# The experts' down product of a mixture-of-experts layer as plain fp32 matmuls from unsplit weights

## What is computed

```
h   = silu(x @ w0[e]) * (x @ w1[e])     # 128 -> 512
y   = h @ wo[e]                         # 512 -> 128
out = sum over the two chosen experts of g * y
x   = layernorm(x + out)
```

## Time and profile before

| | |
|---|---|
| median of 3 runs | 411.37 us (410.9 to 412.04) |
| the profiled execution | span 414.5 us; no other time is recorded for it |
| PE busy | 349.5 us, 84% (weight loads 238.0) |
| DVE busy | 292.3 us, 71% |
| ACT busy | 235.2 us, 57% |
| POOL busy | 230.4 us, 56% |
| granted TensorE clock | 0.98 of full speed over the span |

### The profile page before, as it was taken

The page is one execution under the profiler, slowest core; times in us unless marked ns, Lnnn a source line. Parts: engine busy times, 40 slices in busy tenths (PEclk is TensorE's granted clock), DMA queues, the critical chain, the costliest instruction groups (busy, mean ns, idle before and its releaser), DMA issues.

```text
span 414.5 us, 9020 instructions
## 1 busy us (share of the span) xinstructions
PE 349.5 (84%) x2869; PEld 238.0 (57%) x2869; DVE 292.3 (71%) x836; ACT 235.2 (57%) x460; POOL 230.4 (56%) x341
## 2 busy tenths in 40 slices
PE   1999977888988999988878899988997999999900
PEld 1666645556544545444444445567776899898800
DVE  3555645888788888878796736376776877877737
ACT  2677644432667666455577687744644665666514
POOL 2660598855354435271569788546575445445525
PEclk9999999999999999999999999999999999999975
DMA  8933322636515040322624343211112211111054
GB/s 269 336 110 106 87 85 77 187 94 186 171 33 166 5 140 5 99 70 75 196 69 131 117 155 102 74 32 40 53 41 78 78 53 40 53 52 35 32 171 146
DMA packets 44461, 41.97 MB, mean 101 GB/s; under 512 B 4560, under 2 KB 38416, under 8 KB 44416
## 3 DMA queue, kind: packets, MB, share of 16 engines
q1 hardware_dynamic: 41136, 35.10, 28.1%
q0 software_dynamic: 2272, 4.69, 3.2%
q10 hardware_dynamic: 1008, 1.61, 1.1%
HBM read 26.36 MB, written 14.75 MB: 99 GB/s over the span
## 4 chain that ended last, share of the span: by engine, by line
PE 56%; DVE 20%; issue 7%; POOL 7%; ACT 4%; another core or an unknown queue 3%; DMA 2%; ACTq 0%; DVEq 0%; POOLq 0%
PE banks L1017 12%; DVE nm L1210 8%; PE banks L1044 6%; PE banks L1032 4%; PE banks L859 4%; PE banks L698 4%; PE banks L907 3%; PE banks L1045 2%; PE banks L755 2%; PE banks L937 2%; PE banks L763 2%; DVE ctx_in L1152 2%; PE banks L806 2%; PE banks L934 1%
## 5 line engine op out<-in xcount | busy, mean ns | idle before, releaser
L1210 DVE TENSOR_REDUCE nm<-banks 128x4 f32<-128x1024 f32 x64 | 78.1, 1220 | 17.5 <-PE banks L850 11.4
L1520 ACT ACTIVATE probs_all<-banks 128x1024 f32<-128x1024 f32 x64 | 65.4, 1023 | 36.0 <-PE banks L859 29.6
L1017 PE MATMUL banks<-w_split,scores_in 128*128 x234 | 64.5, 410 | 0.0
L1342 DVE TENSOR_TENSOR ctx_in<-ctx_in,banks 128x512 f32<-128x512 f32 x39 | 26.8, 687 | 27.3 <-ACT ctx_in L1567 21.4
L1017 PEld LDWEIGHTS banks<-w_split,scores_in 128*128 128x128 f32 x234 | 40.8, 189 | 7.7 <-issue 0.9
L1705 POOL DMA_INDIRECT slots_dram<-rows,place_u x32 | 31.9, 996 | 23.5 <-DVE count L1302 16.1
L1727 POOL DMA_INDIRECT y_dram<-x,scatter_u x39 | 38.5, 987 | 11.4 <-POOL x L1723 9.7
L1567 ACT ACTIVATE ctx_in<-banks 128x512 f32<-128x512 f32 x39 | 23.3, 599 | 36.7 <-PE banks L1017 31.9
L859 PE MATMUL banks<-scores_in 32*128 32x256 f32 x256 | 32.2, 326 | 12.0 <-ACT probs_all L1520 6.0
L1044 PE MATMUL banks<-w_split,scores_in 128*128 x156 | 39.1, 327 | 2.8 <-ACT scores_in L1573 2.1
L907 PE MATMUL banks<-probs_all,vals 128*9 128x256 f32 x512 | 39.7, 381 | 0.2
(11 more groups left out here) (230 smaller groups left out, 802.2 us busy)
## 6 DMA issues: line engine op xcount, KB each, us to landing
scores_in<-k_dram SPq DMA_DIRECT2D x32, 128.0 KB, 2.7
scores_in<-q_dram SPq DMA_DIRECT2D x32, 128.0 KB, 2.7
ctx_in<-in_L_ffn_w SPq DMA_DIRECT2D x16, 256.0 KB, 2.7
cs_wide<-cs_dram SPq DMA_DIRECT2D x14, 256.0 KB, 3.7
scores_in<-slots_dram SPq DMA_DIRECT2D x39, 65.0 KB, 1.9
k_dram<-split_qk SPq DMA_DIRECT2D x8, 256.0 KB, 2.5
q_dram<-split_qk SPq DMA_DIRECT2D x8, 256.0 KB, 2.3
ctx_in<-in_L_ffn_wo SPq DMA_DIRECT2D x8, 256.0 KB, 2.9
```

What stands on the lines that cost most here:

```text
L1017: m = TE.matmul(up_bank(i, j), xT[:, i % XT, xh, :], all_weights[:, c + j * FF:][:, bass.ds(expert_at[i], FF)], start=n == 0, stop=n == 2)
L1210: V.tensor_reduce(most, maxima_of(n).rearrange("p (j k q) -> p j k q", j=2, k=TPS), AX_X, ALU.max, negate=True).then_inc(s["nmax"], 1)
L1520: C.activation(probs(n).rearrange("p j k q -> p (j k q)"), EXPS, ACT.Exp, scale=SCALE).then_inc(s["probs"], 1)
```

## The change

Only w0 and w1 are split (16 pieces); wo is loaded as it is, by a DMA for each expert into a buffer of its own (`load_down` into `w_down`), in the steps in which (n - 32) % 3 is 2, so that a step either splits a piece or loads a wo. The hidden is transposed and copied once, unsplit, by ACT; DVE's copy of the rest is gone. `down` is 4 plain fp32 matmuls of 128 columns, and waits for all of `w_down`. DVE makes the tile's result in one operation from the bank: times g, plus x2 out of `xg`; ACT's and POOL's operations are gone, and POOL only scatters. Before the last three `down`, `turn_hidden` of the last tile comes first. `hsT` has a buffer of its own.

```diff
-W_HEAD, W_REST, W_OUT, W_ALL = 0, 2 * FF, 4 * FF, 6 * FF
+W_HEAD, W_REST = 0, 2 * FF
+UP_ALL = 4 * FF // FF
 W_RING = NT * D // FF
-PIECES = 3 * NE
+PIECES = 2 * NE
 XG, AHEAD = 8, 4
-LAST_ADDED = SLOT_TILES - 3
 XT, TURNED_AHEAD, DOWN_LAG, HS = 3, 2, 3, 3
...
+        if i == SLOT_TILES:
+            second.append(("turn_hidden", i - 1))
         if i >= DOWN_LAG:
             second.append(("down", i - DOWN_LAG))
         if i + TURNED_AHEAD < SLOT_TILES:
             second.append(("turn_x2", i + TURNED_AHEAD))
-        if 1 <= i <= SLOT_TILES:
+        if 1 <= i < SLOT_TILES:
             second.append(("turn_hidden", i - 1))
...
-            yield "split_weights", piece
-            if W_RING <= piece + 2 < PIECES:
-                yield "load_weights", piece + 2
-            piece += 1
+        elif n >= LAST_MIXER + 6 and piece + whole_pieces < PIECES + NE:
+            if (n - LAST_MIXER) % 3 == 2:
+                yield "load_down", whole_pieces
+                whole_pieces += 1
+            else:
+                yield "split_weights", piece
+                if W_RING <= piece + 2 < PIECES:
+                    yield "load_weights", piece + 2
+                piece += 1
...
-        w_split = sb("w_split", [P, NE, W_ALL], F32R)
+        w_split = sb("w_split", [P, NE, UP_ALL * FF], F32R)
+        w_down = sb("w_down", [P, NE, FF])
+        hsT = sb("hsT", [P, HS, FF])
...
-            y, turned = bank(6 + i % 2)[:, 0:2 * D], bank(6 + i % 2)[:, 2 * D:3 * D]
+            y, turned = bank(6 + i % 2)[:, 0:D], bank(6 + i % 2)[:, D:2 * D]
...
-                q.wait_ge(s["y_x2"], i - XG + 1)
+                q.wait_ge(s["y_add"], i - XG + 1)
...
+            def load_down(e):
+                mixer_left()
+                SY.dma_start(w_down[:, e, :].rearrange("p (c d) -> p c d", c=FC),
+                             A["L0_ffn_wo"][e].rearrange("(c p) d -> p c d", p=P)).then_inc(a["w_down"], 16)
...
-                                      all_weights[:, c + j * FF:][:, bass.ds(expert_at[i], FF)], start=n == 0, stop=n == 2)
+                                      all_up[:, c + j * FF:][:, bass.ds(expert_at[i] * UP_ALL, FF)], start=n == 0, stop=n == 2)
...
             def down(i):
-                slot = i % HS
                 yb, _ = shared(i)
-                q.wait_ge(s["hsT_hi"], i + 1)
-                q.wait_ge(s["hsT_lo"], i + 1)
+                q.wait_ge(s["hsT"], i + 1)
+                q.wait_ge(a["w_down"], 16 * NE)
                 q.wait_ge(s["xT_lo"], min(i + 2 * TURNED_AHEAD + 1, SLOT_TILES))
                 q.wait_ge(s["y_add"], i - 1)
                 for c in range(FC):
-                    w = all_weights[:, W_OUT + 2 * c * D:][:, bass.ds(expert_at[i], 2 * D)]
-                    TE.matmul(yb[:, 0:2 * D], hsT[:, slot, 0, c * P:(c + 1) * P], w, start=c == 0, stop=False)
-                    m = TE.matmul(yb[:, 0:D], hsT[:, slot, 1, c * P:(c + 1) * P],
-                                  all_weights[:, W_OUT + 2 * c * D:][:, bass.ds(expert_at[i], D)],
-                                  start=False, stop=c == FC - 1)
+                    m = TE.matmul(yb, hsT[:, i % HS, c * P:(c + 1) * P], all_down[:, c * D:][:, bass.ds(expert_at[i], D)],
+                                  start=c == 0, stop=c == FC - 1)
                 m.then_inc(s["down_mm"], 1)
...
-            def turn_hidden(i):
-                slot = i % 2
-                q.wait_ge(s["hsT_hi"], i + 1)
-                q.wait_ge(s["down_mm"], i - HS + 1)
-                V.tensor_tensor(hsT[:, i % HS, 1, :], hidden_bank(i), hsT[:, i % HS, 0, :].bitcast(F32),
-                                ALU.subtract).then_inc(s["hsT_lo"], 1)
...
-                q.wait_ge(s["y_half"], i + 1)
+                q.wait_ge(s["down_mm"], i + 1)
+                q.wait_ge(a[f"g{i % XG}"], 16 * (i // XG + 1))
                 q.wait_ge(a[f"y_out{i % Y_RING}"], 16 * (i // Y_RING))
-                V.scalar_tensor_tensor(y_slot[:, i % Y_RING, :], shared(i)[0][:, 0:D], xg[:, i % XG, ROW_WEIGHT:ROW], y_half[:, i % 2, :],
+                V.scalar_tensor_tensor(y_slot[:, i % Y_RING, :], shared(i)[0], xg[:, i % XG, ROW_WEIGHT:ROW], xg[:, i % XG, 0:D],
                                        ALU.mult, ALU.add).then_inc(s["y_add"], 1)
-                if i >= LAST_ADDED:
-                    y = y_slot[:, i % Y_RING, :]
-                    q.wait_ge(s["y_add"], i + 1)
-                    V.tensor_tensor(y, y, xg[:, i % XG, 0:D], ALU.add).then_inc(s["y_last"], 1)
 
...
-                e, i = divmod(n, 3)
-                raw = w_raw[:, n % W_RING, :]
-                if i < 2:
-                    head = w_split[:, e, W_HEAD + i * FF:W_HEAD + (i + 1) * FF]
-                else:
-                    raw = raw.rearrange("p (c d) -> p c d", c=FC)
-                    head = w_split[:, e, W_OUT:].rearrange("p (c h d) -> p c h d", c=FC, h=2)[:, :, 0, :]
+                e, i = divmod(n, 2)
                 q.wait_ge(a[f"e{n % W_RING}"], 16 * (n // W_RING + 1))
-                C.activation(head, raw, ACT.Identity).then_inc(s["w_hi"], 1)
+                C.activation(w_split[:, e, W_HEAD + i * FF:W_HEAD + (i + 1) * FF], w_raw[:, n % W_RING, :],
+                             ACT.Identity).then_inc(s["w_hi"], 1)
...
-                C.activation(hsT[:, i % HS, 0, :], hidden_bank(i), ACT.Identity).then_inc(s["hsT_hi"], 1)
-
-            def down(i):
-                q.wait_ge(s["down_mm"], i + 1)
-                q.wait_ge(s["y_add"], i - 1)
-                q.wait_ge(a[f"g{i % XG}"], 16 * (i // XG + 1))
-                C.activation(y_half[:, i % 2, :], shared(i)[0][:, D:2 * D], ACT.Identity, scale=xg[:, i % XG, ROW_WEIGHT:ROW]).then_inc(s["y_half"], 1)
+                C.activation(hsT[:, i % HS, :], hidden_bank(i), ACT.Identity).then_inc(s["hsT"], 1)
...
-                y = y_slot[:, i % Y_RING, :]
-                if i < LAST_ADDED:
-                    q.wait_ge(s["y_add"], i + 1)
-                    G.tensor_tensor(y, y, xg[:, i % XG, 0:D], ALU.add).then_inc(s["y_x2"], 1)
-                    q.wait_ge(s["y_x2"], i + 1)
-                else:
-                    q.wait_ge(s["y_last"], i - LAST_ADDED + 1)
+                q.wait_ge(s["y_add"], i + 1)
                 G.indirect_dma_start(
                     y_dram[:, :], bass.IndirectOffsetOnAxis(ap=scatter_u[:, i:i + 1], axis=0),
-                    y, None).then_inc(a[f"y_out{i % Y_RING}"], 16)
+                    y_slot[:, i % Y_RING, :], None).then_inc(a[f"y_out{i % Y_RING}"], 16)
 
             G.memset(minus_half[:, :], -0.5).then_inc(s["consts_g"], 1)
```

More of the change, by code:

```diff
@@ L266, in middle_order @@
 def middle_order():
-    piece = 0
+    piece = whole_pieces = 0
     for n in range(FIRST_STEP, NPAIR):
@@ L293, in middle_order @@
                 yield "load_weights", i
-        elif n >= LAST_MIXER + 6 and piece < PIECES:
-            yield "split_weights", piece
-            if W_RING <= piece + 2 < PIECES:
-                yield "load_weights", piece + 2
-            piece += 1
+        elif n >= LAST_MIXER + 6 and piece + whole_pieces < PIECES + NE:
[7 more added lines that the diff above has]
+                piece += 1
         yield from tiles_step(n)
@@ L327 @@
     "r2 ln2_var ln2_in ln2 x2 x2_t x2T rows_x2 gate_mm logit ge topped chosen rank_mm counted w_hi w_lo "
-    "xg_t xT_hi xT_lo up_mm sil hid turn_mm hsT_hi hsT_lo down_mm y_half y_add y_x2 y_last "
+    "xg_t xT_hi xT_lo up_mm sil hid turn_mm hsT down_mm y_add "
     "end_var end_in end_scaled end_ln out_act out_dve"
@@ L472, in build @@
         w_raw = work.rearrange("p (r n) -> p r n", n=FF)
-        y_slot, y_half = x1[:, 0:Y_RING, :], x1[:, Y_RING:Y_RING + 2, :]
-        to_slots = x1[:, Y_RING + 2, 0:SLOT_TILES]
+        y_slot = x1[:, 0:Y_RING, :]
+        to_slots = x1[:, Y_RING, 0:SLOT_TILES]
         flat_q = scores_in[:, :, :, :].rearrange("p n r s -> p (n r s)")
@@ L1005, in expert_of @@
                 q.wait_ge(s["steps_v"], tile_ready(i))
[L1006 removed]
+                expert_at[i] = TE.value_load(tile_at[0:1, 0, i:i + 1], min_val=0, max_val=(NE - 1) * FF)
             def up(i):
@@ L1027, in turn_hidden @@
                 q.wait_ge(s["av_hi"], B)
-                q.wait_ge(s["hsT_lo"], i if i < TURNED_ALONE else i - 1)
+                q.wait_ge(s["hsT"], i if i < TURNED_ALONE else i - 1)
                 if i == TURNED_ALONE:
@@ L1380, in vector_program @@
                           rank_tiles=rank_tiles, place_tiles=place_tiles,
-                          up=up, turn_hidden=turn_hidden, turn_x2=turn_x2, down=down)
+                          up=up, turn_x2=turn_x2, down=down)
             for stage, *at in middle_order():
```

39 lines of the change are left out of this document (15 added, 24 removed).

## The result

The changed kernel takes 405.26 us in the median of 4 runs (404.54 to 405.73), the kernel before 411.55 (410.9 to 412.04, 4 runs): a ratio of 0.9842, 95% interval 0.9827 to 0.9858, some 6.3 us less. I had forecast 410.4 with a range down to 408.4. Some executions of each kernel run with a lower granted clock and take over 1.5% longer; the ratios here leave them out, the medians in us do not.

The account below looks back on a forecast made before the run. The prediction took TensorE to bound the loop's steady part. Its terms, +0.8 - 0.75 - 0.3 - 0.7 = -0.95 us, turned the median of 411.37 into 410.4 us, range 408.4 to 412.4.

Parts of the forecast that it names:

- Product: `down` in each of 39 turns: eight records take 0.89 us, 0.02 more than before, +0.8 us in all.
- Rivals C: `down`: first weight load not issued ahead under `up`, 0.1 us per turn, +3.9 us, 414.3; chance 0.08.
- D: `down`: bound by columns, not weight loads; 128 more per chunk cost +9.8 us, 419.4; chance 0.03.
- Start of the loop: First 14 tiles: two waits of TensorE on DVE and ACT shrink, -0.75 us together, bounds 0 and -2.
- the wait before L947: TensorE near 295 us, waiting for DVE's table behind the 0.68 us subtraction: the 0.5 us wait goes.
- the 0.25 us at 313 us: ACT leaves a stall with L1579 at 313.28; without L1579, `down` at 314.48 starts 0.25 us sooner.
- Weights: Splitting steps: ACT and POOL lose eight pieces each and buffers fill earlier, -0.3 us, bounds 0 and -2.
- the ring: Four weight buffers delay ACT, 1.4 us in all, 0.42 before an exponential; with 16 pieces they fill earlier.
- The steady part: Loop bound by TensorE: work taken off DVE, ACT and POOL is covered there and worth nothing.
- End: Last tiles: POOL's scatters, 1.26 us apart, set the pace; the last starts at 394.3, -0.7 us, bounds -1.4 and 0.
- Rivals A: Late completions near 287 and 310 us shrink as POOL's queue clears sooner, 1.7 us less, 408.7; chance 0.26.
- B: Late completions grow as POOL's scatters come closer together, +1.5 us, 411.9; chance 0.13.

Follow-up runs that it names:

- the last run with nine buffers: Changed kernel with POOL's additions of x2 back for tiles 0 to 35 and nine buffers of gathered rows for eight, repeated: 425.44 us, ratio 1.0104.
- the second run with ACT's pieces alone: Changed kernel with eight more splitting pieces on ACT (0.63 us each), none on POOL, repeated on a chip without stalls: 407.59 us, ratio 0.9885.

## Why the prediction was wrong

- **Product**: +0.8 forecast, about -0.3 measured (39 turns of 0.007). The 0.89 us for `down` was right; that `up` and the transposes beside it would get shorter was not seen, and why they do stays open. Rivals C (0.1 us per turn) and D (columns) are excluded: the turn did not grow.
- **Start of the loop**: -0.75 forecast, -0.65 measured, and the wait before L947 is gone as said. That the sizes agree is in part luck: the subtraction, meant to be 0.5 of it, gave back 0.20, and the 0.25 us at 313 us was read from a stall.
- **Weights**: -0.3 forecast with a bound of -2, -3.24 measured. This is the step that failed. "ACT's pieces lie mostly in the gap between two exponentials" was nearly right, 0.33 us. The 8 x 1.27 us that POOL loses were given no price beyond the ring, and no reason why not. DVE waited for POOL, by its reads (POOL's pieces alone are 1.11 us, with ACT's 2.20), and ACT did, through the ring of four buffers: its wait was given as 1.4 us in all with 0.42 before an exponential, in a trace with stalls; without stalls one wait alone is 1.62. Even the bound of -2 did not reach.
- **The steady part**: nothing forecast outside `down`, -1.0 found. "It is late next anyway" looked at ACT, DVE and POOL and left out SP, whose load of tile 14 waited for POOL's addition of tile 6. The diff names that wait; the forecast did not follow the queue that it stands in.
- **End**: -0.7 forecast, -0.80 measured, of which 0.59 stand in the last scatter's start behind the last `up` (8.38 to 7.79 us), by POOL's pace as argued; the reordering did not help in it.
- **Rivals A and B** had 0.39 together, all on stalls that the timed runs did not have. The text noted that the profiled execution was 3.1 us slower than the median, and did not ask which part of it was slower. It was more than that: the 3.1 sets a span beside a device time, and in these runs the device time of an execution is 1.3 us above its span (404.54 for 403.2 after the change).

So the sign was right, and the size was off by the weights, 2.9 us, SP's load, 1.0, and the product, 1.1.

## What to carry to other kernels

An engine without a waiter can still hold up another one: look for short operations whose longest instance is several times the shortest, and see what POOL does then. For each wait that a change moves from one semaphore to another, read who is queued behind it, the DMA queues too. Where the profiled execution stands some microseconds off the timed median, find the stretches that make it so before any rival is built on them.

## What was unexpected of the hardware

Two kinds of chip: the same kernel takes 411.5 to 412.1 us on two of them and 418.8 to 420.0 on three. Each was seen on one occasion, so chip and occasion cannot be told apart. In nine of the ten profiles from the slower three the granted clock also falls to 0.50 of full at least once before the loop ends, for 3.4 to 20.5 us; 14 of the 19 falls come just behind a stall. In the last run with nine buffers, 2.31 us of stall come at 236.5 us; after that the clock granted is (third column from the right) 0.56 and 0.50 of full, the lower level, with TensorE busy throughout, until about 262 us:

```profile
225.00:235.00 10.00, 8.19 (x101) 4.63 (x97) 8.12 (x23) 7.18 (x12) 5.08 (x6) 1.00 0.59 168
...
240.00:250.00 10.00, 10.00 (x53) 4.13 (x56) 1.49 (x3) 5.60 (x9) 5.24 (x6) 0.56 0.51 146
250.00:260.00 10.00, 10.00 (x54) 4.80 (x55) 3.21 (x18) 3.59 (x4) 3.23 (x5) 0.50 0.22 75
260.00:270.00 10.00, 9.98 (x85) 5.62 (x84) 4.01 (x24) 6.08 (x9) 7.82 (x8) 0.92 0.12 33
```

It makes 107 matmuls there in 20 us, against 101 in the 10 us before. The first `up` of that run starts at 276.4 us, where the base has 262.0. A fall before any stall of its execution was seen twice, near 124 us in the profiles of the run with the old order and of the second run with ACT's pieces alone: in the latter 0.50 from 125 to 135 us, behind 5 us in which TensorE was busy for 3.65. It is why that profile's span is 410.8 and not why the run's exponentials shift after 200 us.
